# A graph network on one core: the last half product by blocks with its residual in PSUM, and the input's first chunk loaded alone

## What is computed

```python
u, v = x, v_node_feats
for _ in range(3):
    v = mlp(adj @ u, uv_W1, uv_b1, uv_W2, uv_b2, uv_W3, uv_b3)   # leaky_relu(h @ W + b), three times
    u = mlp(adj @ v, vu_W1, vu_b1, vu_W2, vu_b2, vu_W3, vu_b3)
x = layernorm(x + v)                     # the last u is not used
x = layernorm(x + adj @ (x @ gcn_W))
```

## Time and profile before

| | |
|---|---|
| time, median of 3 runs | 1157.84 us (1157.8 to 1158.52) |
| the profiled execution | 1157.88 us, of which the span 1155.9 us |
| busy | PE 99%, PEld 83%, ACT 63%, DVE 62%, POOL 0% of the span |
| the chain that ended last | PE 99% |
| one visit of six matmuls, later in the chain | 126 records in 28.57 us at 402.76 us, so 1.361 us for six |
| granted clock of PE | 1.00 in all 40 slices of the page, 0.999 over the span |
| DMA | 281.42 MB, mean 243 GB/s; 384, 387 and 365 GB/s in the first three slices of 28.9 us |

### The profile page before, as it was taken

How to read it: one execution, slowest core, us unless ns; L and a number is a source line. 1 busy time by engine, 2 the same in 40 slices (tenths; PEclk the granted TensorE clock), 3 DMA queues, 4 the chain that set the end, 5 groups by cost and what they waited for, 6 DMA issues and landing times.

```text
span 1155.9 us, 14073 instructions
## 1 busy us (share of the span) xinstructions
PE 1149.8 (99%) x5314; PEld 961.3 (83%) x5314; DVE 721.2 (62%) x837; ACT 726.6 (63%) x925; POOL 4.2 (0%) x12
## 2 busy tenths in 40 slices
PE   9999999999999999999999999999999999999998
PEld 8888888888888888888888888888888888888887
DVE  6987545554665344765553585545558775459996
ACT  6876654455776444876554486544567874459884
POOL 0000000000000000000000000000000000000000
PEclk9999999999999999999999999999999999999999
DMA  9997656645855576666553584656558565579990
GB/s 384 387 365 274 231 197 244 229 178 195 319 185 207 190 276 234 242 231 255 218 182 145 196 349 182 224 197 234 198 196 327 206 230 191 216 274 371 373 382 22
DMA packets 39361, 281.42 MB, mean 243 GB/s; under 512 B 4416, under 2 KB 4800, under 8 KB 5632
## 3 DMA queue, kind: packets, MB, share of 16 engines
q1 hardware_dynamic: 38736, 278.69, 64.1%
q0 software_dynamic: 560, 1.84, 0.4%
HBM read 278.41 MB, written 2.10 MB: 243 GB/s over the span
## 4 chain that ended last, share of the span: by engine, by line
PE 99%; DVE 0%; issue 0%; ACT 0%; DVEq 0%
PE acc L960 90%; PE proj L900 4%; PE layer L869 1%; PE layer L866 1%; PE layer L867 1%; PE proj L975 0%; PE acc L893 0%; PE proj L893 0%; PE layer L893 0%; DVE stats L791 0%; DVE h L787 0%; DVE h L749 0%; DVE part L811 0%; ACT std L656 0%; DVEq L307 0%
## 5 line engine op out<-in xcount | busy, mean ns | idle before, releaser
L960 PE MATMUL acc<-high,p_low 128*128 128x512 f32 x1544 | 603.0, 391 | 0.0
L960 PE MATMUL acc<-high,p_high 128*128 128x512 f32 x1544 | 598.9, 388 | 0.0
L728 DVE TENSOR_TENSOR low<-raw,high 128x1024 fp32r<-128x1024 f32 x482 | 562.2, 1218 | 47.5 <-ACT high L571 46.8
L571 ACT ACTIVATE high<-raw 128x1024 fp32r<-128x1024 f32 x482 | 485.9, 1054 | 70.9 <-PE acc L960 49.0
L960 PE MATMUL acc<-low,p_high 128*128 128x512 f32 x1544 | 473.8, 388 | 0.0
L960 PEld LDWEIGHTS acc<-low,p_high 128*128 128x128 f32 x1544 | 289.1, 188 | 60.1 <-DVE low L728 0.5
L960 PEld LDWEIGHTS acc<-high,p_high 128*128 128x128 f32 x1544 | 290.1, 188 | 58.1
L960 PEld LDWEIGHTS acc<-high,p_low 128*128 128x128 f32 x1544 | 290.0, 188 | 57.8
L754 DVE TENSOR_TENSOR h_low<-h,h_high 128x512 fp32r<-128x512 f32 x40 | 27.6, 690 | 223.4 <-ACT h L624 223.4
L623 ACT ACTIVATE h_high<-acc,consts 128x512 fp32r<-128x512 f32 x40 | 27.5, 686 | 165.0 <-PE acc L960 165.0
L765 DVE TENSOR_TENSOR p_low<-proj,p_high 128x512 fp32r<-128x512 f32 x32 | 22.1, 690 | 64.1 <-ACT p_high L647 64.1
(11 more groups left out here) (60 smaller groups left out, 333.4 us busy)
## 6 DMA issues: line engine op xcount, KB each, us to landing
raw<-adj_dram SPq DMA_DIRECT2D x241, 1024.0 KB, 5.5
late<-adj_dram SPq DMA_DIRECT2D x16, 1024.0 KB, 7.4
early<-adj_dram SPq DMA_DIRECT2D x4, 1024.0 KB, 11.7
input<-x_dram SPq DMA_DIRECT2D x1, 2048.0 KB, 11.3
out_dram<-part POOLq DMA_DIRECT2D x7, 256.0 KB, 6.5
input<-x_turned_dram SPq DMA_DIRECT2D x1, 1024.0 KB, 6.9
input<-x_turned_dram SPq DMA_DIRECT2D x1, 576.0 KB, 4.1
input<-x_turned_dram SPq DMA_DIRECT2D x1, 512.0 KB, 4.9
```

The costliest lines, as they stand in the source:

```text
L571: nc.scalar.activation(high[t % SLOTS][:], raw_of(t), ACT.Copy).then_inc(high_ready, 1)
L728: nc.vector.tensor_tensor(low[t % SLOTS][:], raw_of(t), high[t % SLOTS][:].bitcast(F32), ALU.subtract).then_inc(low_ready, 1)
L960: return nc.tensor.matmul(bank[:, into], p[parity][:, block(j)], a[slot][:, columns(j)], start=(first and n == s.opens and s.seed < 0), st ...
```

## The change

At the start the input comes in four pieces of 1, 1, 2 and 4 chunks. Of the first (weight and chunk 0) SP loads the partitions 0 to 63 and ACT's own queue the partitions 64 to 127, ahead of ACT's table load. There are 7 warming matmuls in place of 9. The first band is loaded as two halves, and tile 0 waits for its own half alone. `X_SPLIT` puts chunks 4 to 7 of `p_high` and `p_low` ahead of tile 5, 7, 9 and 11.

At the end the sum of the second half goes on in the bank of the large sum, in place of a bank of its own, so nothing of `part` is added to it; `keep` takes 256 columns. DVE copies the two blocks of the second half to SBUF one by one, and PE multiplies each as it comes. ACT has put the residual of both halves into PSUM before (`seed_residuals`: first half into `layer0`, block 2 into `layer1`, block 3 into `proj`), and PE adds to it (`start=False`). DVE then measures in PSUM, without the add, and both normalizations read PSUM. The inverse of the first half stands one step earlier.

```diff
-X_PIECES = [2, 2, 4]
-X_SPLIT = [0, 0, 0, 0, 2, 4, 6, 8]
+X_PIECES = [1, 1, 2, 4]
+X_SPLIT = [0, 0, 0, 0, 5, 7, 9, 11]
-WARMING = 9
+WARMING = 7
-HALF_PROJECT, HALF_MEASURE, HALF_ROOT, HALF_INVERT, HALF_NORMALIZE = 2, 3, 4, 5, 6
+HALF_PROJECT, HALF_MEASURE, HALF_ROOT, HALF_INVERT, HALF_NORMALIZE = 2, 3, 4, 4, 5
...
+            if s.continues >= 0:
+                s.bank = self.sums[s.continues].bank
...
+                rows = slice(0, D if piece else D // 2)
+                sp.dma_start(input_and_weight[rows, columns], x_turned[rows, columns]).then_inc(x_loaded[piece], 16)
...
+                if t == 0:
+                    sp.dma_start(raw_of(0), band[:, 0:TILE]).then_inc(first_loaded, 16)
+                    sp.dma_start(raw_of(1), band[:, TILE:]).then_inc(band_loaded[buffer], 16)
...
+            rows, columns = slice(D // 2, D), slice(0, D + X_PIECES[0] * CHUNK)
+            nc.scalar.dma_start(input_and_weight[rows, columns], x_turned[rows, columns]).then_inc(x_loaded[0], 16)
...
+            def seed_residuals():
+                last = len(chunks) - 1
+                residual = resid[:, blocks_of(sum_of(last).chunk)]
...
+                nc.scalar.activation(layer[0][:, columns_in(0)], residual[:, columns_in(0)], ACT.Copy).then_inc(residual_seeded, 1)
+                for j in blocks_in(last):
+                    nc.scalar.activation(block_in(shown(last)[j], j), block_in(residual, j), ACT.Copy).then_inc(residual_seeded, 1)
...
+                if s.half == 0:
+                    nc.vector.tensor_tensor(h[i % 2][:, columns], acc[s.bank][:, columns], part_of(s.chunk)[:, columns],
+                                            ALU.add).then_inc(half_ready, 1)
+                else:
+                    for j in blocks_in(i):
+                        nc.vector.tensor_copy(block_in(h[i % 2], j), block_in(acc[s.bank], j)).then_inc(half_ready, 1)
...
+                for nth, j in enumerate(blocks_in(i)):
+                    if half == 1:
+                        pe.wait_ge(half_ready, half + 1 + nth)
+                    done = nc.tensor.matmul(block_in(shown(i)[j], j), block_in(h[i % 2], j), w["gcn_W"], start=False,
+                                            stop=True, skip_group_check=True)
```

More of the change, by code:

```diff
@@ L238, in last_sweep @@
         columns = self.band(rows)
-        self.one(rows[-1], columns[:-IN_HALVES], self.open(LAST, rows[-1], "keep"))
+        whole = self.open(LAST, rows[-1], "keep")
+        self.one(rows[-1], columns[:-IN_HALVES], whole)
         last = [self.tile(rows[-1], column) for column in columns[-IN_HALVES:]]
@@ L243, in last_sweep @@
             self.sums[total].half = half
+            self.sums[total].continues = whole if half else -1
             for t in last:
@@ L469, in blocks_in, with shown @@
             return range(IN_CHUNK) if half < 0 else range(half * IN_CHUNK // 2, (half + 1) * IN_CHUNK // 2)
+        def shown(i):
+            if chunks[i].half < 0:
+                return [h[i % 2]] * IN_CHUNK
+            return [layer[0], layer[0], layer[1], proj]
         def measured(i):
@@ L588, in keep @@
                     act.wait_ge(first_stored, 16)
-                nc.scalar.activation(part_of(s.chunk), acc[s.bank][:], ACT.Copy).then_inc(part_kept, 1)
+                columns = columns_in(0 if (s.product, s.chunk) == (LAST, sum_of(len(chunks) - 1).chunk) else -1)
+                nc.scalar.activation(part_of(s.chunk)[:, columns], acc[s.bank][:, columns], ACT.Copy).then_inc(part_kept, 1)
+            def seed_residuals():
+                last = len(chunks) - 1
+                residual = resid[:, blocks_of(sum_of(last).chunk)]
+                act.wait_ge(second_ready, FINAL)
+                act.wait_ge(third_ready, NORM)
+                act.wait_ge(normed_ready, CHUNKS)
+                act.wait_ge(x_added, last - 1 - NORM)
+                nc.scalar.activation(layer[0][:, columns_in(0)], residual[:, columns_in(0)], ACT.Copy).then_inc(residual_seeded, 1)
+                for j in blocks_in(last):
+                    nc.scalar.activation(block_in(shown(last)[j], j), block_in(residual, j), ACT.Copy).then_inc(residual_seeded, 1)
             def seed(s):
@@ L703, in _ @@
                             gather(i)
+                        if n == chunk.start - 4 and chunk.half == 0:
+                            seed_residuals()
                         if n == place(i, LAST_ROOT, HALF_ROOT):
@@ L785, in measure @@
                         dve.wait_ge(std_ready, i - NORM)
[L786 to L789, removed]
+                if chunks[i].half < 0:
+                    nc.vector.tensor_tensor(h[i % 2][:], source[:], resid[:, blocks_of(sum_of(i).chunk)],
+                                            ALU.add).then_inc(x_added, 1)
+                    dve.wait_ge(x_added, i - NORM + 1)
                 for j in blocks_in(i):
-                    nc.vector.bn_stats(stats[:, j, :], block_in(h[i % 2], j)).then_inc(stats_ready, 1)
+                    if chunks[i].half == 1:
+                        dve.wait_ge(proj_done, i + 1 + blocks_in(i).index(j))
+                    nc.vector.bn_stats(stats[:, j, :], block_in(shown(i)[j], j)).then_inc(stats_ready, 1)
                 for nth, j in enumerate(blocks_in(i)):
@@ L810, in normalize_half @@
                 for j in blocks_in(i):
-                    done = nc.vector.tensor_scalar(block_in(part_of(sum_of(i).chunk), j), block_in(h[i % 2], j),
+                    done = nc.vector.tensor_scalar(block_in(part_of(sum_of(i).chunk), j), block_in(shown(i)[j], j),
                                                    moments[:, j, 0:1], rstd[:, j:j + 1], op0=ALU.subtract, op1=ALU.mult)
@@ L897, in turning @@
             def turning(i, source, weight):
-                for j in blocks_in(i):
+                for j in range(IN_CHUNK):
                     done = nc.tensor.matmul(block_in(proj, j), block_in(source, j), weight, start=True,
@@ L919, in project @@
             def project(i):
[L920 to L923, removed]
+                pe.wait_ge(total_ready, i - FINAL + 1)
                 if i > FINAL:
@@ L960, in add @@
                     return nc.tensor.matmul(bank[:, into], p[parity][:, block(j)], a[slot][:, columns(j)],
-                                            start=(first and n == s.opens and s.seed < 0), stop=(last and n == s.closes),
-                                            skip_group_check=s.seed >= 0)
+                                            start=(first and n == s.opens and s.seed < 0 and s.continues < 0), stop=(last and n == s.closes),
+                                            skip_group_check=s.seed >= 0 or s.continues >= 0)
                 for j in range(PER_TILE):
@@ L986, in _ @@
                             turn(i)
-                    elif n == place(i, PROJECT, HALF_PROJECT):
+                    elif chunk.half < 0 and n == chunk.start + PROJECT:
                         project(i)
+                    elif chunk.half >= 0 and n == chunk.start + HALF_PROJECT:
+                        project_half(i)
                 if n < len(visits):
```

29 lines of the change are left out of this document (21 added, 8 removed).

## The result

The changed kernel takes 1159.53 us (median of 22 runs, 1158.94 to 1160.59), the kernel before 1157.89 (22 runs, 1157.67 to 1158.52): a ratio of 1.0014, 95% interval 1.0008 to 1.0019. The span grew from 1155.9 to 1157.5 us.

The account below looks back on a forecast made before the run. PE was taken to bound the kernel (busy 1149.8 of 1155.9 us). From 1157.88, 0.2 lost at the start and 0.87 gained at the end gave 1157.21, forecast 1157.2; range 1156.2 to 1158.1.

Parts of the forecast that it names:

- the first chunk's: Start: halves on two queues land near 4.2 us, at latest 4.84; extra issues on SP and ACT cost nothing.
- Rival 3: Late `low` stream: band 3 or next bands over 0.7 us later, passed to PE; 1158.3 at 1.1 later; chance 0.12.
- the signs I named: Last projection near 12.6; DVE idle before `low` 2 and 6, then none to `low` 11; PE's load waits; shorter tail.
- The warming: PE's start: two matmuls fewer end warming 0.94 us earlier, near 4.3; projections end 0.45 us sooner, near 12.65.
- X_SPLIT: DVE's first row: three chunks before `low` 11 instead of one; visit 11 comes 0.2 us later instead of 0.45 earlier.
- The loads behind `low` 11: Load for tiles 18 and 19 goes out 0.8 us later, covered by 0.8; taken as 0, bounds 0 and 0.4.
- The end: Second half behind PE's last visit: aggregation ends 0.82 to 0.92 us sooner, taken as 0.87.
- Stats from PSUM: Second half's end: reading statistics from PSUM instead of SBUF priced at zero, bound 0.1 us.
- The hand-overs: Second half's end: PE starts the last block 0.06 us after DVE's copies, at 1150.81; stats at 1151.34.
- normalizing from PSUM: End, two blocks: 0.60 us as from SBUF, so zero cost; the skill's rule would give 0.13 more, forecast 1157.3.
- The inverse ahead of the copies: First half's inverse before DVE's critical copy: fits by 0.04 us; slip taken as 0, bound 0.2.
- The residual into PSUM and the shorter `keep`: ACT before `keep`: three copy instructions, at most 1.8 us, fit in 2.90 us idle; free.

Follow-up runs that it names:

- the fastest kernel: Changed end, input pieces 1, 3, 4 on one queue, 7 warming matmuls, first band whole, chunks 4 to 7 of p early: 1156.72 us, ratio 0.9990 to before.
- the late order alone: Chunks 4 to 7 of p ahead of tiles 5, 7, 9 and 11, against the kernel with old start and changed end (1157.23 us): 1157.25 us.

## Why the prediction was wrong

**The step that failed** is the first chunk's, and in it one sentence: the extra issue on SP and the one on ACT "both cost nothing". I priced the transfers by their bytes at 384 GB/s and took every later landing as before. The small piece was nearly as I said (4.45 against 4.2). But what came behind landed 1.9 (chunks 2 and 3 of x) to 2.4 us (band 1) later, which my bounds of 0.5 us did not hold. The loss is not one thing: 256 KB in short rows (1.5 us alone), halves of 64 partitions (1.0 alone), the halved band (0.2 alone). They overlap, so that taking one out gains 0.1 to 0.5. For the halves no run tells the 64 partitions from the issue on a second queue: wherever ACT issued, both were changed.

**Rival 3 is what happened**, by an earlier band than the one I had named. It had the late stream of `low` decide, each tenth going to PE as DVE has no idle time. Band 3 came only 1.5 us late (20.7 against 19.2); band 1 came 2.4 late, and from there on (16.93) DVE had no pause. The load for visit 11 stood at 30.96, 1.9 us behind the 29.05 at which I had `low` 11 ready. With that, and 0.2 less at the end, my sum gives 1157.2 + 1.9 + 0.2 = 1159.3; the profiled run took 1159.25. Of the signs I named, DVE idle before `low` 2, none from there to `low` 11 and a weight load that waits for it came; the last projection ended at 14.37, not near 12.6. I gave this rival 0.12 because the bytes were the same; they were, but not their shape. The section on the 64 partitions stood in the Trainium skill ("SBUF — State Buffer"), and I had weighed the other one, on issuing engines.

**The warming** was right in size, partly by luck. With pieces 1, 3, 4 it is worth 1157.13 - 1156.72 = 0.41 us (0.45 forecast). But I had the rise fixed near 6.5 and four more records slow before it. It was not fixed: in the changed kernel all eight records of chunk 0 were already fast (1.16 us from 4.51), while before six were slow. In the fastest kernel chunk 0 was done at 5.50, and chunk 1 started at 5.63, just behind the landing of its piece near 5.5, so there the landing held PE.

**X_SPLIT** was right in mechanism and too large. PE did wait for `low` 11, 0.28 us in the changed kernel and 0.28 with pieces 1, 3, 4. I had priced it at 0.6 us. Between the medians it was 0.37 where the visits start early, a part of which may be the landing, and 0.0 where they start at 12.9. In that last trace the bands had landed 0.3 us sooner than before, which was the condition I named. In the changed kernel it was worth nothing: in either order the stream that starts with band 1 decided.

**The loads behind `low` 11** I took as free. In the two traces where the start was early and the order late (the late order alone, and the one with pieces 1, 3, 4) PE's weight load waited once more, at 39 us, 0.4 and 0.3 us for `h_low`, and 0.2 to 0.3 us more are left behind visit 11 than the usual 1128.3. In the same kernels with the early order no load waits there. That it was the loads and not DVE's late stream itself is not shown.

**The end** gained 0.67 us by the medians; I said 0.87. The trace has 0.67 up to the aggregation but 0.55 up to the normalization, so the equal numbers are chance: 0.14 us of the medians' gain lie outside the span (time less span is 1.78 us with the changed end, 1.92 before), and no row shows why. Stats from PSUM cost nothing, as priced (0.30 and 0.28 us). The hand-overs were mis-sized: PE began 0.15 us behind the first copy and 0.24 behind the second, where I had 0.06 from one pair of rows, and the stats 0.10 behind PE's last record. And **normalizing from PSUM**, which I priced at zero against the Trainium skill's rule ("VectorE: DVE Perf Modes", "Why PSUM operands drop a tier"), took 0.73 us for two blocks in place of 0.60: 0.13, the estimate from that page of the Trainium skill. My ground against it, that 343 ns is longer than 282 ns of a two-source operation, compared two different operations.

**The inverse ahead of the copies** cost nothing: the copy began 0.09 us behind the last visit, as the add had done, with the shift ending 0.05 us before. The residual into PSUM and the shorter `keep` were hidden, as said.

## What to carry to other kernels

Cutting a load at the head of a queue to get its first part sooner was free here only where the pieces kept all 128 partitions and no 256 KB piece of 2048 B rows stood among them; price a transfer by its shape, and look at where the transfers behind it land, not only at the piece. When bands feed an engine that never waits, a lead at the start is given back by whatever is late next, so check the next landing before counting it. And a value left in PSUM to save an add can cost part of it back when a one-source DVE operation reads it.

## What the runs showed of the hardware

- Two transfers of 64 partitions with rows of 8 KB ran at 242 GB/s at a full busy share, against 414 to 445 for 128 partitions in the same trace.
- With a transfer of 64 partitions issued on ACT beside one on SP, the first issue on SP took 0.56 us in place of 0.38, and the first bytes moved 0.5 us later. Whether the second queue or the 64 partitions do it is open: two issues of 64 partitions on SP alone took 0.55 and 0.59 us, of 128 partitions 0.43.
- Behind a 256 KB piece of 128 rows of 2048 B that stood second or third in the queue, what followed was slower in three kernels, down to 283 GB/s even with one transfer of 1536 KB behind. The cause stays open; so does why a band in column halves (rows of 4 KB) falls to 272 GB/s while x in 512 KB pieces with rows of 4 KB does not.
- Where PE waited 4.28 us for the 1536 KB piece behind one of them its granted clock fell to 0.50, the lower of its two levels (1.2 of 2.4 GHz), when it went on: 32 records then took 4.64 us in place of 3.57. The rows have records, clock, DMA share and rate:

```profile
8.00:10.00 2.00, 0.00 (x0) 1.00 0.99 406
...
12.00:14.00 2.00, 2.00 (x11) 0.50 1.02 430
```

- A transfer's costly shape can't be read from the busy share alone: 285 and 439 GB/s show 0.98 and 1.06. The two losses also look different: with 64 partitions of 8 KB rows the share is full (1.10 at 242 GB/s), with the 256 KB piece the engines are in part idle (0.84 at 252 GB/s).
